# Attention: the score products of the narrow diagonal key blocks, issued once and issued twice

## What is computed

```python
q = (x @ Wq.T + bq).reshape(b, l, h, hd).transpose(0, 2, 1, 3)   # b 2, l 1024, h 32, hd 16
k = (x @ Wk.T + bk).reshape(b, l, h, hd).transpose(0, 2, 1, 3)
v = (x @ Wv.T + bv).reshape(b, l, h, hd).transpose(0, 2, 1, 3)
scores = jnp.einsum('bhqd,bhkd->bhqk', q, k) / math.sqrt(hd)
causal = jnp.tril(jnp.ones((l, l), bool))
scores = jnp.where(causal, scores, -jnp.inf)
att = jax.nn.softmax(scores, axis=-1)
out = jnp.einsum('bhqk,bhkd->bhqd', att, v)
```

## Time and profile before

| | |
|---|---|
| median of 3 runs | 4300.12 us (4286.41 to 4308.26) |
| the profiled execution | 4294.83 us, its span 4293.1 us |
| mean granted TensorE clock, as a share of 2.4 GHz | 0.907 |
| TensorE busy | 3861.4 us, 90% of the span, 18056 matmuls |
| VectorE, ScalarE, GpSimd busy | 2711.2, 1695.2, 1880.8 us |

### The profile page before, as it was taken

One profiled execution on the slowest core, in us unless ns is written; L12 is line 12 of the kernel. 1 busy time (PEld: TensorE's weight loads), 2 busy tenths in 40 slices (PEclk: granted clock), 3 DMA queues, 4 the chain that ended last, 5 costly groups with the idle time before them and its releaser, 6 DMA issues.

```text
span 4293.1 us, 61464 instructions
## 1 busy us (share of the span) xinstructions
PE 3861.4 (90%) x18056; PEld 2813.5 (66%) x18056; DVE 2711.2 (63%) x5034; ACT 1695.2 (39%) x3538; POOL 1880.8 (44%) x2017
## 2 busy tenths in 40 slices
PE   7899799689999999979878896996899999999797
PEld 4444478567777777757654444885677777777576
DVE  3567445577777777764435673555777777777644
ACT  1344411355545555541113444113555555555411
POOL 1111344355555655654311113443555556655542
PEclk8677899899999999989977767998999999999899
DMA  3221011011100111001032210110101001110010
GB/s 73 36 36 31 24 51 45 22 33 30 32 20 25 34 32 29 22 15 45 35 81 36 36 32 29 46 45 22 35 28 32 20 25 34 32 29 22 15 52 35
DMA packets 81456, 145.59 MB, mean 34 GB/s; under 512 B 16392, under 2 KB 18520, under 8 KB 81264
## 3 DMA queue, kind: packets, MB, share of 16 engines
q1 hardware_dynamic: 81264, 143.28, 12.9%
HBM read 113.08 MB, written 4.19 MB: 27 GB/s over the span
## 4 chain that ended last, share of the span: by engine, by line
PE 69%; issue 11%; DVE 7%; ACT 4%; POOL 3%; DVEq 2%; POOLq 2%; DMA 1%; SPq 1%; ACTq 0%
PE banks L492 15%; PE banks L493 14%; PE banks L494 14%; PE banks L832 4%; PE banks L671 4%; PE banks L652 3%; PE banks L628 3%; PE banks L825 2%; PE banks L845 2%; DVE conv L1344 2%; DVEq L1347 1%; PE banks L767 1%; PE banks L768 1%; POOL X L1509 1%; ACT conv L1005 1%
## 5 line engine op out<-in xcount | busy, mean ns | idle before, releaser
L1344 DVE SCALAR_TENSOR_TENSOR conv<-banks,cpar,conv 128x509 f32<-128x509 f32 (+2 forms) x576 | 428.2, 744 | 115.3 <-ACT conv L1005 100.9
L948 ACT ACTIVATE probs<-banks 128x1024 f32<-128x1024 f32 (+3 forms) x384 | 297.7, 810 | 309.4 <-PE banks L652 308.9
L1172 DVE TENSOR_TENSOR Y<-banks,Y 128x512 f32<-128x512 f32 x400 | 276.1, 691 | 188.1 <-PE banks L494 187.9
L1608 POOL TENSOR_SCALAR_AFFINE_SELECT probs<-probs 128x256 f32<-128x256 f32 x256 | 104.2, 408 | 645.8 <-ACT probs L948 645.5
L628 PE MATMUL banks<-stack_k,stack_q 48*128 48x512 f32 (+3 forms) x768 | 331.7, 502 | 59.3 <-DVEq L1218 19.8
L1672 POOL TENSOR_TENSOR state<-state,gt 128x512 f32<-128x512 f32 x112 | 133.5, 1192 | 500.4 <-PE banks L825 500.4
L492 PE MATMUL banks<-xhi,f_hi 128*128 128x512 f32 x800 | 322.6, 403 | 3.5 <-DVE xlo L1143 3.5
L492 PE MATMUL banks<-xhi,wx_hi 128*128 128x512 f32 x768 | 312.0, 406 | 14.4 <-DVE conv L1344 14.4
L493 PE MATMUL banks<-xhi,f_lo 128*128 128x512 f32 x800 | 319.9, 400 | 0.0
L494 PE MATMUL banks<-xlo,f_hi 128*128 128x512 f32 x800 | 319.4, 399 | 0.0
L494 PE MATMUL banks<-xlo,wx_hi 128*128 128x512 f32 x768 | 306.0, 398 | 0.0
(11 more groups left out here) (209 smaller groups left out, 10185.0 us busy)
## 6 DMA issues: line engine op xcount, KB each, us to landing
m_raw<-in_w_mamba SPq DMA_DIRECT2D x224, 256.0 KB, 2.6
f_raw<-in_w_ffn SPq DMA_DIRECT2D x50, 768.0 KB, 4.5
stack_q<-part_hi SPq DMA_DIRECT2D x128, 64.0 KB, 2.4
stack_k<-part_hi SPq DMA_DIRECT2D x128, 64.0 KB, 2.5
X<-in_x SPq DMA_DIRECT2D x4, 1024.0 KB, 6.5
wqk_raw<-in_w_attn SPq DMA_DIRECT2D x8, 512.0 KB, 3.5
stack_q<-part_lo SPq DMA_DIRECT2D x64, 64.0 KB, 2.4
stack_k<-part_lo SPq DMA_DIRECT2D x64, 64.0 KB, 2.5
```

The costliest lines, as they stand in the source:

```text
L948: act.activation(probs[n % 2][:, 2 * p:2 * p + 2, 0:w], banks[:, 2 * p:2 * p + 2, 0:w], ACT.Exp, scale=1.0 / HD ** 0.5).then_inc(exp_done[ ...
L1172: dve.tensor_tensor(Y[:, i, :], bank[6 + i % 2], Y[:, i, :], ALU.add).then_inc(f["dn_used"], 1)
L1344: r = dve.scalar_tensor_tensor(out=rest, in0=src[:, 0:HALF - lag], scalar=cpar[:, o:o + 1], in1=rest, op0=ALU.mult, op1=ALU.add)
```

## The change

In the narrow steps each score product is issued twice, one directly behind the other, with the same operands and into the same bank; `start=True` makes the second write over what the first left. Only the second of an odd head signals st_done. Nothing else is different, on any engine.

```diff
-                        r = pe.matmul(bank[h][:, 0:HALF - lo],
-                                      stack_k[buf][base:base + ROWS + 2, h, j * P:(j + 1) * P],
-                                      stack_q[buf][base:base + ROWS + 2, h, s * HALF + lo:(s + 1) * HALF],
-                                      start=True, stop=True)
+                        for _ in range(2 if lo else 1):
+                            r = pe.matmul(bank[h][:, 0:HALF - lo],
+                                          stack_k[buf][base:base + ROWS + 2, h, j * P:(j + 1) * P],
+                                          stack_q[buf][base:base + ROWS + 2, h, s * HALF + lo:(s + 1) * HALF],
+                                          start=True, stop=True)
                         if h % 2:
                             r.then_inc(st_done[h // 2], 1)
```

## The result

The changed kernel took 4323.12 us (median of 12 runs, 4311.59 to 4335.38), the kernel before 4301.55 us (median of 12, 4286.41 to 4313.05). The ratio is 1.0048, with a 95% interval from 1.0034 to 1.0063: half a per cent slower, inside the class "within 0.5%" and at its edge, for the interval reaches past it. The forecast was 4303 us, the range 4270 to 4338. The profiled execution took 4318.62 us, its span 4316.9 us, 23.8 us more than the span before.

The account below looks back on a forecast made before the run. TensorE, busy for 90% of the span, was taken as the bound, with its clock often low in the attention. Direct cost 14 less 11 for the clock gave +3 us: 4298 profiled, 4303 us as a median, range 4270 to 4338.

Parts of the forecast that it names:

- Step 10: In turns with pieces, two added 384-wide step products fit the 0.18 us idle ahead of the maxima; two of 0.12 don't: +0.2 us.
- Step 9: In turns with pieces, added scores fit before the last piece, which waits for VectorE; 0.1 us for ScalarE's later scores.
- Step 11: Last step of turns with pieces: added scores largely hidden; 0.1 us since ScalarE gets scores later, though nothing waits at once.
- Steps 1 to 3: Low-clock steps of turns with pieces: added scores largely hidden, 0.1 us each for ScalarE getting its scores later.
- Turn 7: Turn without pieces, so less hides the added scores: 2 us each, 4 us for the two turns.
- Direct cost: Added scores not hidden, without the clock: 10 us in the 14 turns with pieces plus 4 in two turns 7, 14 us.
- Clock, -11 us: Clock stays up through steps 1 to 3 in three of 12 turns (1 to 6, twice), gaining 3.7 us each: -11 us.
- Turns 1 to 6 at 0.74 to 0.78: Sign: mean clock expected there in the profile after; the prediction is wrong if it moves by more than 0.06.
- The other sign: Steps 1 to 3 at 1.2 GHz taking more than 12.5 us would show the prediction wrong.
- In series: Slower rival: added scores delay pieces, so VectorE starts later; 4340 us at half, 4374 at all of 74 us; chance 0.23.
- Clock held: Faster rival: added scores keep TensorE at 2.4 GHz over the turn's edge; 4270 us, down to 4223; chance 0.23.
- Nothing on either side: Rival: every added score is covered and no clock fall avoided; 4296 to 4300 us; shares the forecast's 0.54.

Follow-up runs that it names:

- the kernel with all steps: Against the kernel before, all score products issued twice, the full-width ones of steps 0 and 4 to 8 too: 4315.69 us, ratio 1.0046.

## Why the prediction was right, and where it was not

The time lay in the range and in the class, 20 us above the forecast. The range was 68 us wide, and the class was met by a hair. Of the two terms the direct cost was too low, 14 us where 20 to 28 were paid, and the clock's net about right. By its own steps:

- **What the edit is**: right. 384 products with their loads, and no wait moved.
- **Step 10, +0.2 us**: right, +0.24 (2.32 to 2.56). Waits of 0.18 us are filled and the rest is paid, in every kernel that has these twins.
- **Step 9, +0.1**: right, +0.12.
- **Step 11, +0.1**: wrong by four times, +0.43 in the turns 0 to 5 (next to nothing in turn 6). This is the step that failed. It said that ScalarE gets its scores later "though nothing waits for it at once". In the last step of a turn something does: its own values, through exp and mask, as the timelines above show. The kernel with twins in step 11 alone shows the price by itself.
- **Steps 1 to 3, +0.1 each**: right for 2 and 3 at 1.2 GHz (4.33 to 4.45, and 3.57 to 3.68). For step 1 it is mis-sized where the step begins and ends at the low clock. That is so in turn 0: 4.00 us before, 4.69 after. Eight products of 384 columns at 0.32 us are 2.56 us on the scores' half, and the values wait behind the last one. In the other turns it is from nothing to 0.3 us: step 1 of turn 6 took 5.05 us at 0.50 before, in the second batch, and 5.37 at 0.57 after; that of turn 4 took 4.98 us at 0.66 after, and 4.99 at 0.66 in the kernel with twins in 9 to 11 alone.
- **Turn 7, +2 us**: as a direct cost right or a little high. The kernel with twins in steps 9 to 11 pays 1.0 us in it. But turn 7 grew by 7.6 us in each batch, and the prediction looked for clock in turns 1 to 6 alone. Its step 7 takes 4.89 us at 1.2 GHz and 2.89 at 2.4, so a low microsecond there costs 2.00 / 4.89 = 0.41 us, more than the 0.32 of turns 4 and 5, where VectorE has a pace of its own.
- **Direct cost, 14 us**: too low. It was 17 us by the steps (steps 9 to 11 at 0.8 in 12 turns and at 0.4 in two; 1 to 3 at some 0.4 in 12 turns and 0.9 in two), and 2 to 3 for turn 7. By what is left when the clock is taken out it is 21 and 3 in the traced pair, and 28 over all executions. So 20 to 28 us, of which the mis-sized step 11 is 12 x 0.33 = 4; where the rest of the upper figure lies is not shown.
- **Clock, -11 us**: over all executions -9 us, so the size was about right. But it is a net of parts that the prediction didn't foresee. In turns 0 to 6 of the traced pair the credit was 20 us. Steps 1 to 3 ran wholly at 2.4 GHz in turn 5 of both batches (two turns, where three were assumed), and partly in 0, 1 and 4. It was given back there: 28 us x 0.45 = 12.6 us in turn 7 and 7.9 us outside the turns. Net of the pair, about 0; its execution of before was one of the better ones (0.907, where the mean of 60 is 0.904). The 0.45 is that of turn 7's step 6, 2.11 us before and 3.84 us after. That the size came out near is in part luck.
- **Sum**: 3 us predicted; 23 - 20 + 13 + 8 = 24 us in the traced pair, 28 - 9 = 19 us over all executions.
- **Turns 1 to 6 at 0.74 to 0.78**: 0.79 in both batches, 0.01 above that band; it moved by 0.05 and 0.04, inside the 0.06. The other sign did show: the stretch from the fall to the end of step 3 in turn 6 took 12.74 us at 0.50, past the 12.5. Of the 1.16 us over the 11.58 of the earlier trace rows, 0.78 came from a fall that lay earlier in step 1 (0.76 us into it, 1.54 before) and the rest from twins, so the sign mixed two things.
- **The rivals.** In series: no. The upper bound was 74 us and the direct cost some third of it; the last piece of step 9 starts 1.40 us into the step (1.28 before), 0.12 later for four twins of 0.175 ahead of it. Clock held: in single turns only. Nothing on either side: no, the twins were paid for.

That a product waiting for its own half doesn't hold up the other, on which the sum rested in place of the rule in the Trainium skill ("TensorE: Matmul & The Clock Gate", Part 3, "What overlaps and what doesn't"), is borne out: the piece at 323.36 starts 0.28 us ahead of the twin that stands before it in the list, and steps 9 and 2 cost far less than four twins' length. The rule of the same page, section "HAM oscillation", that the fall comes from idle gaps between bursts isn't borne out by the kernel with 64-column twins, where TensorE is busy for all 3.89 us of the step in which the clock falls. Nor does steady work bring it back at once: before, TensorE is busy for 27.19 of the 27.30 us from 369.10 to 396.40, all at 0.50.

**What stays open.** That the twins move the mean clock is shown by all executions, up in some places and down in others. What decides in which turn it falls isn't settled. The columns in the products bear on it (64 or whole twins, all steps or some), and so does something that in some kernels differs between two batches of the same program in one execution. The 7.9 us outside the turns can't be laid to the twins with certainty: in the kernel with all steps the time outside the turns was 4307.6 - 704.2 = 3603.4 us, with step 11 alone 4306.2 - 706.2 = 3600.0 us, before 4293.1 - 688.6 = 3604.5 us, and in the changed kernel 4316.9 - 704.1 = 3612.8 us, one execution each. The part of the direct cost between the 20 us of the steps and the 28 of all executions isn't placed either.

## What to carry to other kernels

Added work on one half of the array is cheap where a later engine is waited for anyway, and dear in the last step of a stretch, whose own results are consumed at once, unless the next stretch waits for something else; so look for each step's next reader, and not for idle time in general. Where the profile shows two clock levels, count the time at the low one in every part of the kernel, the parts without an edit too, and compare like parts within one execution before a difference of that size is laid to the edit. An effect of the clock that is found in one turn is no estimate for the whole: in the traced execution it gave 20 us in one place and took as much in others. The mean clock of every timed execution costs no trace, and it parted the clock's share from the work's where single traces could not.

## What the runs showed that was not expected

- A second product costs the same with 128 and with 64 columns at 2.4 GHz (step 11 of turn 7 takes 2.38 us with either), 0.11 us for each head in step 11 of turn 3. That this is its weight load is argued from that, not seen.
- A product over all 128 rows amid products on halves of the rows takes 0.43 us to the next start at 2.4 GHz (377.31 to 377.74), about as long as a score of 512 columns takes at 1.2 GHz, and 0.23 us was expected by the pace of the scores.
- Cutting the twins from their full width to 64 columns made the kernel 35 us slower (4357.68 and 4323.12 us) while the prices of its steps at 2.4 GHz stayed the same or fell.
- Over 23 executions of one kernel the time follows the time at the low clock at 0.30 us for each microsecond.
- The same turns of the same program differ by up to 25 us between its two batches (352.17 and 377.56 us).
